# Feed-forward stages of a hybrid network: query and key both scaled by their norm on VectorE, and a new order of each engine's work within a step

## What is computed

```python
def _layer(x, wqkv, qs, ksc, wo, lg, lb, w1, b1, w2, b2):
    h = shift_token(x)                       # second half of the features comes from the token before
    q, k, v = split(h @ wqkv)                # 8 heads of 64
    q = l2norm(q) * qs
    k = l2norm(k) * ksc
    q, k = rotary_xpos(q, k)
    o = local_attention(q, k, v)             # windows of 64, each sees itself and the one before; softmax
    x = x + o @ wo
    h = shift_token(x)
    h = layernorm(h) * lg + lb
    a, g = split(h @ w1 + b1)                # 341 + 341
    x = x + (a * gelu(g)) @ w2 + b2
    return x
```

## Time and profile before

| | |
|---|---|
| median of 3 runs | 2710.06 us (2708.85 to 2716.6) |
| the profiled execution | 2707.96 us, its span 2706.2 us |
| TensorE matmul busy | 2168.5 us (80%) |
| TensorE weight load | 1100.5 us (41%) |
| VectorE | 1907.9 us (71%) |
| ScalarE | 1479.2 us (55%) |
| GpSimd | 1010.4 us (37%) |
| mean granted TensorE clock | 0.923 of full speed |

### The profile page before, as it was taken

How to read it: one execution, slowest core, us unless ns; L and a number is a source line. 1 busy time by engine, 2 the same in 40 slices (tenths; PEclk the granted TensorE clock), 3 DMA queues, 4 the chain that set the end, 5 groups by cost and what they waited for, 6 DMA issues and landing times. The chain is left out here.

```text
span 2706.2 us, 45818 instructions
## 1 busy us (share of the span) xinstructions
PE 2168.5 (80%) x16928; PEld 1100.5 (41%) x16928; DVE 1907.9 (71%) x2678; ACT 1479.2 (55%) x3450; POOL 1010.4 (37%) x514
## 2 busy tenths in 40 slices
PE   3543567898989898763999999996689989998987
PEld 1211234555555554321333333332355555555553
DVE  7456567778878878364777777773577877778873
ACT  3343436666666666430355555655466667666663
POOL 1011156666666666100000000002566666666660
PEclk8777779999999999886799999997899999999998
DMA  1000211111111111012011111102111111111111
GB/s 51 0 0 0 82 24 32 40 32 37 32 39 34 36 36 25 23 75 78 29 46 46 40 46 41 45 25 89 28 34 35 33 40 32 40 31 38 32 29 39
DMA packets 91468, 101.15 MB, mean 37 GB/s; under 512 B 13305, under 2 KB 58561, under 8 KB 91125
## 3 DMA queue, kind: packets, MB, share of 16 engines
q1 hardware_dynamic: 90661, 97.16, 13.7%
q0 software_dynamic: 592, 1.12, 0.1%
HBM read 35.98 MB, written 8.39 MB: 16 GB/s over the span
## 5 line engine op out<-in xcount | busy, mean ns | idle before, releaser
L486 ACT ACTIVATE ffn_PB<-ffn_s,ffn_NS,ffn_RN 128x128 f32<-128x128 f32 x1024 | 456.5, 464 | 484.8 <-DVE ffn_NS L608 484.4
L1431 DVE TENSOR_REDUCE attn_b_NX<-attn_b_s 128x1 f32<-128x512 f32 (+3 forms) x608 | 384.6, 659 | 153.5 <-PE attn_b_s L1247 147.8
L1374 ACT ACTIVATE attn_b_PT<-attn_b_s 128x1024 f32<-128x1024 f32 (+3 forms) x352 | 298.6, 870 | 294.8 <-PE attn_b_s L1276 290.4
L708 POOL TENSOR_TENSOR ffn_QK<-ffn_T 128x1024 f32<-128x1024 f32 x128 | 303.2, 2368 | 356.4 <-DVE ffn_T L624 356.4
L714 POOL TENSOR_TENSOR ffn_RN<-ffn_SS,ffn_mhalf 128x16 f32<-128x16 f32 x128 | 372.7, 2912 | 76.2 <-DVE ffn_SS L643 75.9
L702 POOL TENSOR_TENSOR ffn_PB<-ffn_PB,ffn_RDEN 128x1024 f32<-128x1024 f32 x128 | 242.8, 1897 | 179.1 <-DVE ffn_RDEN L600 179.1
L325 PE MATMUL ffn_w<-ffn_Wqkv,ffn_H 128*128 128x512 f32 x512 | 262.9, 638 | 20.3 <-DMA ffn_H<-ffn_Y 14.6
L640 DVE TENSOR_REDUCE ffn_SS<-ffn_SQ 128x16 f32<-128x1024 f32 x128 | 156.2, 1220 | 161.5 <-ACT ffn_SQ L535 161.5
L399 PE MATMUL ffn_m<-ffn_HN,ffn_W 128*114 128x512 f32 x384 | 198.4, 616 | 54.3 <-DVE ffn_AG L568 37.6
L1247 PE MATMUL attn_b_s<-attn_b_KS,attn_b_QS 72*128 72x512 bf16 (+3 forms) x768 | 230.9, 348 | 12.0 <-DVE attn_b_NX L1431 8.8
L486 ACT ACTIVATION_READ_ACCUMULATOR ffn_PB<-ffn_s,ffn_NS,ffn_RN 128x1 f32 x1024 | 215.2, 210 | 0.0
(11 more groups left out here) (202 smaller groups left out, 3939.3 us busy)
## 6 DMA issues: line engine op xcount, KB each, us to landing
ffn_Voff<-ffn_Vcur SPq DMA_DIRECT2D x248, 128.0 KB, 2.3
attn_b_QS<-attn_b_qk_parts SPq DMA_DIRECT2D x192, 48.0 KB
attn_b_KS<-attn_b_qk_parts SPq DMA_DIRECT2D x192, 48.0 KB
ffn_H<-ffn_Y SPq DMA_DIRECT2D x64, 128.0 KB, 2.5
ffn_H<-ffn_U SPq DMA_DIRECT2D x64, 128.0 KB, 2.5
attn_b_qk_parts<-attn_b_RP SPq DMA_DIRECT2D x8, 768.0 KB, 3.5
ffn_rope<-in_ffn_rope_dram SPq DMA_DIRECT2D x4, 1024.0 KB, 11.1
attn_b_rope<-attn_b_OS SPq DMA_DIRECT2D x256, 16.0 KB
```

The lines of the kernel that those rows point to most:

```text
L486: last = act.activation(PB[:, x % 2, e, p, :], s_ps[:, e, p * P:(p + 1) * P], ACT.Exp, bias=NS[:, x % 2, e, p:p + 1], scale=RN[:, x % 4, h ...
L708: pool.tensor_tensor(QK[:, x % 2, :, :, :].rearrange("p c q k -> p (c q k)"), T1[:, :, :, :].rearrange("p c h k -> p (c h k)"), T2[:, :, : ...
L1374: act.activation(PT[:, j % 2, g:g + pack, 0:width], s2_ps[k % 2][:, 0:pack * pitch].rearrange("p (q w) -> p q w", q=pack)[:, :, 0:width], ...
L1431: dve.tensor_reduce(NX[:, m % 2, c, g:g + pack, i], s1_ps[k % 2][:, 0:pack * (hi - lo)].rearrange("p (q w) -> p q w", q=pack), AX_X, ALU.m ...
```

## The change

1. VectorE now multiplies query and key both by RN: one product of 128x1024 instead of 128x512. The exponential has no scale and takes the negated maximum NM as bias; NS and its instruction are gone. RN is 2 deep instead of 4, and the power waits for the multiplication of two tiles before.
2. Each engine's statements within a step stand in another order. TensorE: value1, projection of query and key, attention times V, gate2, projection of V, value0, scores, w2, centre, value2, turn of the probabilities, gates 1 and 0, turn of query and key, wo, mean. ScalarE: gelu phase, variance, square, attention output, V, second square, all eight exponentials, query copy. VectorE: residual U, hide 2, hide 0, reciprocal, rope products, HN, hide 1, multiplication, maximum, w2's result, probabilities, residual X, sum of squares, key copy. GpSimd keeps its order.
3. The MLP's chunks have other places in a group and another order: gates 1, 0, 2 and values 2, 1, 0.

The core of the diff:

```diff
-        RN = sb("RN", [P, 4, 2 * NH])
+        RN = sb("RN", [P, 2, 2 * NH])
-        NS = sb("NS", [P, 2, 2, NPAIR])
...
-            ahead = {"gate2": (0, 2), "value01": (0, 2), "value2": (0, 2), "wo": (1, 1), "centre": (2, 1),
-                     "mean": (2, 1), "w2": (3, 2), "gate01": (3, 1)}
+            ahead = {"gate2": (0, 2), "value2": (0, 2), "value1": (1, 2), "value0": (1, 2), "wo": (1, 1),
+                     "centre": (2, 1), "mean": (2, 1), "w2": (3, 2), "gate10": (3, 1)}
...
             for i in STEPS:
-                if real(i):
-                    score(i)
-                g = mlp_at(i, "gate2")
-                if g is not None:
-                    pe.wait_ge(gelu, 3 * g + 1)
-                    hidden(g, 1, 2)
+                g = mlp_at(i, "value1")
+                if g is not None:
+                    pe.wait_ge(gelu, 3 * g + 3)
+                    hidden(g, 0, 1)
                 if real(i + 2):
                     project_qk(i + 2)
                 if real(i - 2):
                     attend(i - 2)
+                g = mlp_at(i, "gate2")
+                if g is not None:
+                    pe.wait_ge(gelu, 3 * g + 2)
+                    hidden(g, 1, 2)
                 if real(i + 2):
                     project_v(i + 2)
...
+                g = mlp_at(i, "value0")
+                if g is not None:
+                    pe.wait_ge(hid, 3 * g + 1)
                     hidden(g, 0, 0)
...
+                if real(i):
+                    score(i)
...
+                if real(i - 1):
+                    turn_probs(i - 1)
+                g = mlp_at(i, "gate10")
+                if g is not None:
+                    pe.wait_ge(hn, g + 1)
+                    if g % NT == 0:
+                        pe.wait_ge(s_w1, g // NT + 1)
+                    if g >= 1:
+                        pe.wait_ge(ynext, g)
+                    hidden(g, 1, 1)
+                    hidden(g, 1, 0)
                 if real(i + 1):
                     turn(i + 1)
-                if real(i - 1):
-                    turn_probs(i - 1)
...
                 for p in range(NPAIR):
-                    h = 2 * p + e
                     last = act.activation(PB[:, x % 2, e, p, :], s_ps[:, e, p * P:(p + 1) * P], ACT.Exp,
-                                          bias=NS[:, x % 2, e, p:p + 1], scale=RN[:, x % 4, h:h + 1],
+                                          bias=NM[:, x % 2, e, p:p + 1],
                                           accum_out=DEN[:, x % 2, e, p:p + 1])
...
-                if real(i):
-                    exps(i, 0)
                 if real(i + 2):
                     x = i + 2
...
+                    act.wait_ge(roped, x + 1)
+                    if x >= 1:
+                        act.wait_ge(sumsq, x)
+                    act.activation(SQ[:, :, :, :].rearrange("p c h e -> p c (h e)"), w0_ps[:, :, :], ACT.Square)\
+                       .then_inc(squared, 1)
...
+                if real(i):
+                    exps(i, 0)
+                    exps(i, 1)
                 if real(i + 1):
                     x = i + 1
                     act.wait_ge(turned, 2 * x + 1)
...
-                    k = QK[:, x % 2, 1, :, :].rearrange("p q (e k) -> p (q e) k", k=DH)
-                    dve.tensor_tensor(k, k, RN[:, x % 4, NH:2 * NH].unsqueeze(2).broadcast_to([P, NH, DH]), ALU.mult)\
-                       .then_inc(k_scaled, 1)
...
+                g = mlp_at(i, "value1")
+                if g is not None:
+                    hide(g, 1)
+                if real(i + 1):
+                    x = i + 1
+                    dve.wait_ge(rope_sum, x + 1)
+                    dve.wait_ge(rnorm, x + 1)
+                    qk = QK[:, x % 2, :, :, :].rearrange("p c q (e k) -> p (c q e) k", k=DH)
+                    dve.tensor_tensor(qk, qk, RN[:, x % 2, :].unsqueeze(2).broadcast_to([P, 2 * NH, DH]), ALU.mult)\
+                       .then_inc(scaled, 1)
+                if real(i):
+                    dve.wait_ge(scores, i + 1)
+                    if i >= 2:
+                        dve.wait_ge(probs, 2 * i - 2)
+                    dve.tensor_reduce(NM[:, i % 2, :, :], s_ps[:, :, :].rearrange("p e (q k) -> p e q k", k=P),
+                                      AX_X, ALU.max, negate=True).then_inc(negmax, 1)
...
                     pool.wait_ge(clamped, x + 1)
-                    if x >= 4:
-                        pool.wait_ge(probs, 2 * (x - 4) + 2)
-                    pool.tensor_tensor(RN[:, x % 4, :], SS[:, x % 2, :], mhalf[:, :], ALU.pow).then_inc(rnorm, 1)
+                    if x >= 2:
+                        pool.wait_ge(scaled, x - 1)
+                    pool.tensor_tensor(RN[:, x % 2, :], SS[:, x % 2, :], mhalf[:, :], ALU.pow).then_inc(rnorm, 1)
```

More of the change, by code:

```diff
@@ L434, in _ @@
                     last.then_inc(w2_mm, 1)
+                g = mlp_at(i, "centre")
+                if g is not None:
+                    pe.wait_ge(u, g + 1)
+                    pe.wait_ge(s_h2[g % 2], 32 * (g // 2 + 1))
+                    pe.matmul(m_ps[:, 0, :], keep["centre"][:, :], H2[:, :], start=True, stop=True).then_inc(centre_mm, 1)
+                g = mlp_at(i, "value2")
+                if g is not None:
+                    pe.wait_ge(gelu, 3 * g + 1)
+                    hidden(g, 0, 2)
+                if real(i - 1):
[9 more added lines that the diff above has]
+                    hidden(g, 1, 0)
                 if real(i + 1):
                     turn(i + 1)
-                if real(i - 1):
-                    turn_probs(i - 1)
-                g = mlp_at(i, "value2")
-                if g is not None:
-                    pe.wait_ge(hid, 3 * g + 1)
-                    hidden(g, 0, 2)
                 g = mlp_at(i, "wo")
@@ L572, in _ @@
             for i in STEPS:
-                g = mlp_at(i, "centre")
+                g = mlp_at(i - 1, "wo")
                 if g is not None:
@@ L625, in _ @@
                     last.then_inc(roped, 1)
-                g = mlp_at(i - 1, "value2")
-                if g is not None:
-                    hide(g, 2)
                 g = mlp_at(i - 1, "mean")
@@ L677, in _ @@
                     dve.tensor_tensor(xs, xs, z, ALU.add).then_inc(x_added, 1)
+                if real(i + 2):
+                    x = i + 2
+                    dve.wait_ge(squared, x + 1)
+                    if x >= 2:
+                        dve.wait_ge(rnorm, x - 1)
+                    dve.reduce_sum(SS[:, x % 2, :], SQ[:, :, :, :].rearrange("p c h e -> p (c h) e"), AX_X)\
+                       .then_inc(sumsq, 1)
+                    dve.wait_ge(sumsq, x + 1)
+                    dve.tensor_scalar(SS[:, x % 2, :], SS[:, x % 2, :], 1e-24, None, ALU.max).then_inc(clamped, 1)
+                if real(i + 1):
+                    x = i + 1
+                    l, t, b = place(x)
+                    dve.wait_ge(turned, 2 * x + 2)
+                    if x >= NB:
+                        dve.wait_ge(scores, x - NB + 1)
+                    else:
+                        dve.wait_ge(s_zero, 2)
+                    dve.tensor_copy(KT[:, b, :, :, t % 2, :],
+                                    w1_ps[:, 1, :].rearrange("p (q h c) -> p q h c", q=NPAIR, h=2)).then_inc(kt, 1)
             dve.wait_ge(x_added, NT)
```

100 lines of the change are left out of this document (24 added, 76 removed).

## The result

| | before | after |
|---|---|---|
| median | 2711.11 us (4 runs) | 2545.36 us (4 runs, 2544.68 to 2553.45) |
| ratio to before | | 0.939, 95% interval 0.937 to 0.942 |
| the profiled execution | 2707.96 us | 2544.68 us, its span 2542.7 us |
| TensorE matmul busy | 80% | 84% |
| VectorE | 71% | 76% |

The change makes the kernel 6.1% faster, 163.3 us between the two profiled executions. The forecast was 130.6 and its range ended at 2550: the direction and the new bound (TensorE) were right, the size was a fifth too small, and the time fell 5 us outside the range.

What follows compares the result with a forecast made beforehand. A loop of waits, no full engine, was taken as the bound. Full groups save 53.3 and first steps 12, 65.3 per stage, 130.6 for two: 2707.96 becomes 2577.4, the median 2580 us; range 2550 to 2610, chance 0.70.

Steps and rivals of the forecast that it cites:

- the four exponentials ahead of the square: ScalarE's queue in the old loop: they and two copies delay the square, closing a loop of 11.16 us per step.
- walk (b): GpSimd's loop: from the multiplication's start the power ends at 8.0 us, scaling at 10.0; the power no longer waits for exponentials.
- Its sign: Mark of being right, on ScalarE: the square comes within 0.5 us of the rope products' end.
- The size of the group: Full group of four steps: floor of 41.9 plus 0.5 of waits, 42.4 us, saving 4.1 per group.
- two ends: TensorE's work per group: 41.1 us summed from pieces, 41.9 from busy time; the latter was used as floor.
- The waits: TensorE's idle time per full group: about 0.4 in step 0, 0.1 in steps 1 and 3, none in 2; 0.5 taken.
- The start: First 8 steps of each stage: plain step 10.0 against 11.4, 1.5 saved per step, 12 us (bounds 8 and 20).
- the walk: VectorE against GpSimd: multiplication first where nothing precedes it; in steps 1 and 3 it meets the scaling, waiting 0 to 2.4 us.
- the marks I gave: Signs of the collision: multiplication's median 1.2 with a tail to 3.6, rope sum 3.5 in half of its instances.
- Rival 1: Multiplication meets GpSimd's rope sum in steps 1 and 3, TensorE idles: 43.9 to 44.2 per group, 2630 us; chance 0.18.
- Rival 2: GpSimd's queued instruction goes first, so the multiplication waits for scaling and rope sum: 48.5 per group, 2778 us; chance 0.07.
- Rival 3: Another loop keeps the old pace, such as scores waiting for eight exponentials: 11.1 to 11.6 per step, 2710 us; chance 0.05.

Runs made afterwards that it cites:

- e8: The kernel after with the multiplication moved back ahead of the reciprocal and the rope products, its old place: 2754.9 us, 1.015 of before.
- e3: The kernel after with one more TensorE product per group, the centring matmul done twice into the same bank: 2578.2 us, 0.951 of before.
- e5: The kernel after with the multiplication on the key only, 512 wide, the query's norm left out (cost alone): 2540.6 us, 0.936 of before.
- e12: The kernel after with ScalarE's second table load later and TensorE's turn of query and key ahead of gates 1 and 0: 2532.2 us, 0.934 of before.
- e11: The kernel after with ScalarE's second table load moved behind the square and two copies of that step: 2536.0 us, 0.936 of before.
- e6: The kernel after with a scale operand, a column of ones, in the exponential again: 2557.8 us, 0.943 of before.
- e9: The kernel after with GpSimd's power replaced by a product of the same operands (norm wrong, cost alone): 2591.3 us, 0.956 of before.
- e2: The kernel after with NS, the exponential's scale and the 512-wide multiplication kept, so only the new order: 2589.1 us, 0.956 of before.
- e4: The kernel after with one more VectorE copy per tile, the turned key also into a scratch tile: 2576.0 us, 0.951 of before.
- e7: The kernel after with ScalarE's first four exponentials put ahead of the square again: 3132.4 us, 1.155 of before.

## Why the prediction was right or wrong

**The bound before: right. The link that was cut: wrong.** A loop of waits through the power set the pace, and it is gone: the shift is no longer among the waits, and the power is early. But the prediction closed the loop through the four exponentials ahead of the square. In its own row the rope products have ended at 732.9 and the square starts at 733.26, so they held it back by 0.4 us. e8 shows that with the square first and the multiplication at its old place the power stands in the loop again (11.54). The prediction's walk (b) had the right path all the same, since it starts at a multiplication behind the rope products; it gives ScalarE's order the credit. Its sign, a square within 0.5 us of the rope products' end, would have held in most steps of the kernel before as well. After the change the square follows 0.03 behind them, but 1.8 in the gelu step.

**TensorE as the new bound of the full groups: right.** It is busy 41.54 of 41.67 us; e3 and e5 show it by load.

**The size of the group: wrong, 42.4 for 41.67.** This is the step that failed, worth 0.73 x 26 = 19 us. The term that was mis-sized is the floor of TensorE's work, 41.9 where e12 shows 41.06. I had two ends, 41.1 from the starts of the matmuls and 41.9 from busy time, and took the upper. The same TensorE instructions have 41.88 of busy time in a group with 4.6 us of waits, 41.54 after the change, 41.36 in e11 and 41.10 in e12 with none. I read this from the records' ends: at each wait the 0.16 us that the next matmul would have covered counts as busy. The starts were right, e12's group of 41.06 against my 41.1, but not to that digit: the pieces as I listed them make 6.7 of attention work per step and not 6.8 to 6.9. By the starts in e12 a group holds 27.7 of attention work and 13.4 of the MLP's, where I had 27.4 and 13.7, and the two errors cancel.

The waits were put at 0.5 and were 0.6 (41.67 - 41.06), and this agreement is luck in part. I took nothing for the exponential's scale operand, within 0.1 per four. It is 0.3 per four, 0.63 per step, and e6 shows that it is worth 0.24 per group. With the exponential that I reckoned with, the waits would have been 0.85 (41.91 - 41.06).

**The start: half wrong.** Tiles 0 to 8 gave 12.0, as forecast, from another mixture: the plain step is 9.53 and not 10.0, and two of the eight steps take 10.6 and 11.5. The steps before tile 0 have the multiplication behind the rope products as well and gave 4.9 that I had counted as nothing, 10 us in two stages. A part of that may be TensorE's clock, which was 0.83 from 356 us to tile 0 and had been 0.70; this was not separated. The tail gave 1.7 where I had 0, plus or minus 1.

So 19 + 10 + 3 = 32 us are missing, and 2577.4 - 32 = 2545. The range failed for a reason of its own: its arithmetic gave 2542 for the floor and the best start, and I cut it to 2550. The 41.6 in it is not my lower floor either: with 41.1 and the best start the end would have been near 2530.

**The collision: right in kind, and in the main where the walk said.** In steps 1 and 3 the multiplication meets the scaling, not the rope sum, and takes 1.71 and 2.11, at most 2.84. It meets it in step 0 as well (1.56), where the walk had VectorE there first; only step 2 has 1.22. Its median is 1.71, not the 1.2 of the marks I gave; the rope sum is at 3.3 nearly always, not in half of its instances, since it is queued behind the multiplication in steps 1 and 3 too. None of this is on TensorE's path in the full groups: e12 has the same collisions (1870 ns as a mean) and TensorE never waits. In the plain steps the multiplication's wait for the scaling is a part of the loop of 9.53. The page "SBUF — State Buffer" of the Trainium skill, section "Who interferes with whom", has issue order decide who blocks; here both orders appear in one step, multiplication behind scaling and rope sum behind multiplication, and each ran only when the other's instruction had ended.

**The rivals.** Rival 1's cause did not arise, but e9 brought it about and its size was right: 43.70. Rival 2 fell: wherever both engines had the next instruction ready, they took turns. Rival 3, an old pace kept by another loop, fell: the plain step is 9.53 and not over 11.

**Left open.** How e2's 0.96 divides between NS and the rest, and why e4's 2.7 us cost 1.2 and not less was not traced to single waits, and for e12 it was not tried whether VectorE is then the next bound.

## What to carry to other kernels

Sum the distances between starts, not the busy times, when an engine's floor is wanted: busy time held 0.8 us more than the starts in 41.9, and that was more than half of the miss. Before crediting one wait with a loop, look at what else ends just before it: the square had two predecessors 0.4 us apart, and the prediction named the wrong one. When an instruction moves to where it can collide with another engine, ask which of that engine's instructions it will meet, and what sets that: here a slow power protects the kernel, and making it 2.7 us faster cost 46 us. When listing a loop, follow the queue of every engine that it passes, for both loops that I got wrong ran through an engine that I had skipped.

## What the runs showed of the hardware that was not expected

- A per-partition scale operand in ScalarE's exponential of 128x128 float32 costs about 80 ns: 385 ns without and 464 to 470 with it. The page "ScalarE: Activation LUTs" of the Trainium skill, section "What ACT_TABLE_LOAD costs", gives about 93 ns for each such operand; the runs here agree to within 15 ns, and the prediction had taken nothing for it.
- GpSimd's power on 128x16 elements takes 2910 ns, a product of the same operands 221.
- TensorE's clock: in e7, whose turn came after a wait of 5.5 us in a step of 14.16, the granted clock was 0.76 over 50 us and 0.50 during the turn, and eight turns took 1.94 instead of 1.04 us.
